# Local maxima of a tile taken in two halves of two score banks, in a kernel of local and routed attention

## The reference

```python
xn = layernorm(x)
# local attention: 16 query heads, 4 key/value heads, rms norm and rope on q and k
q, k, v = xn @ Wq.T + bq, xn @ Wk.T + bk, xn @ Wv.T + bv
q, k = rope(rmsnorm(q, qn_w)), rope(rmsnorm(k, kn_w))
scores = q k^T * scale;  masked where key > query or query - key > 64
local = softmax(scores) v @ Wo.T + bo
# routed attention: one of 16 k/v heads is picked per token by a gate
gating = softmax(xn @ W_gate.T);  idx = argmax(gating);  top = max(gating)
fq, fk, fv = split(xn @ W_qkv.T)
k_shared, v_shared = fk[idx], fv[idx] * top
routed = causal softmax(fq k_shared^T / sqrt(32)) v_shared
out = x + local + routed
```

## Time and profile before

| | us |
|---|---|
| median of 3 runs | 668.64 (667.66 to 670.04) |
| profiled execution, its own time | 671.4 |
| its span | 669.5 |
| PE busy | 637.4 (95%) |
| DVE busy | 455.8 (68%) |
| POOL busy | 442.4 (66%) |
| ACT busy | 361.7 (54%) |
| granted PE clock, mean | 0.993 of full |

### The profile page before, as it was taken

One profiled execution on the slowest core, in us unless ns is written; L12 is line 12 of the kernel. 1 busy time (PEld: TensorE's weight loads), 2 busy tenths in 40 slices (PEclk: granted clock), 3 DMA queues, 4 the chain that ended last, 5 costly groups with the idle time before them and its releaser, 6 DMA issues.

```text
span 669.5 us, 19210 instructions
## 1 busy us (share of the span) xinstructions
PE 637.4 (95%) x7432; PEld 509.8 (76%) x7432; DVE 455.8 (68%) x1184; ACT 361.7 (54%) x906; POOL 442.4 (66%) x384
## 2 busy tenths in 40 slices
PE   4699999999999999999999899999999999999997
PEld 3587788887888888888778677777777777777675
DVE  3966457657665675656664388887878787878454
ACT  5357355625544445535257455656565565656684
POOL 3876856368654749382895467776878687868730
PEclk9999999999999999999999899999999999999999
DMA  9524222241223133212216631503214131302011
GB/s 315 197 60 112 60 77 79 76 122 41 78 70 91 50 94 104 78 39 75 64 33 166 163 96 58 137 26 93 71 51 113 51 111 36 104 29 89 4 34 33
DMA packets 64939, 56.59 MB, mean 85 GB/s; under 512 B 6480, under 2 KB 48848, under 8 KB 64848
## 3 DMA queue, kind: packets, MB, share of 16 engines
q1 hardware_dynamic: 62704, 54.45, 27.9%
q10 hardware_dynamic: 2144, 0.93, 0.5%
HBM read 37.20 MB, written 17.89 MB: 82 GB/s over the span
## 4 chain that ended last, share of the span: by engine, by line
PE 88%; DVE 5%; ACT 2%; DMA 2%; issue 2%; SPq 0%; ACTq 0%; DVEq 0%
PE gemm L946 20%; PE s_ps L1055 12%; PE od_ps L1104 11%; PE st_ps L1088 10%; PE gemm L1032 7%; PE gemm L942 6%; PE od_ps L1118 5%; PE win L1006 4%; PE win L991 3%; PE s_ps L1127 2%; PE av L1018 2%; DMA raw<-w_tok 2%; PE av L1045 1%; PE tp L957 1%; PE tp L913 1%
## 5 line engine op out<-in xcount | busy, mean ns | idle before, releaser
L946 PE MATMUL gemm<-w_tok,xt 128*128 128x512 f32 (+1 forms) x768 | 184.0, 380 | 5.4 <-DVE g_exp L1188 2.2
L946 PEld LDWEIGHTS gemm<-w_tok,xt 128*128 128x128 f32 x768 | 129.6, 191 | 28.5 <-DVE g_exp L1188 2.7
L1055 PE MATMUL s_ps<-k_stack,w_tok 96*128 96x512 f32 (+2 forms) x336 | 100.0, 381 | 0.3 <-DVE x_res L1286 0.3
L1088 PE MATMUL st_ps<-w_tok,k_stack 98*128 98x512 f32 x288 | 98.9, 413 | 0.2 <-ACT p_loc L1545 0.2
L1545 ACT ACTIVATE p_loc<-st_ps 128x512 f32<-128x512 f32 x144 | 77.6, 599 | 35.9 <-PE st_ps L1088 34.7
L1321 DVE TENSOR_REDUCE picked_fk<-s_ps 128x1 f32<-128x512 f32 x112 | 72.3, 684 | 9.0 <-PE s_ps L1055 8.9
L1497 ACT ACTIVATE p_loc<-win,l_max 128x96 f32<-128x96 f32 x256 | 60.9, 390 | 31.1 <-DVE l_max L1260 31.1
L1055 PEld LDWEIGHTS s_ps<-k_stack,w_tok 96*128 96x128 f32 x336 | 54.9, 188 | 24.6 <-issue 8.8
L1642 POOL TENSOR_TENSOR rope_b<-qkv,sin_t 128x128 f32<-128x128 f32 (+1 forms) x32 | 27.5, 880 | 65.5 <-DVE qkv L1238 65.5
L1666 POOL TENSOR_TENSOR p_loc<-p_loc,l_rec 128x1536 f32<-128x1536 f32 x16 | 44.1, 2758 | 36.4 <-DVE l_rec L1272 36.4
L1324 DVE CUSTOM_DVE_ANT_0 s_ps<-s_ps,x_ln,picked_fk 128x128 f32<-128x128 f32 (+3 forms) x112 | 56.8, 555 | 9.7 <-PE s_ps L1055 9.7
(11 more groups left out here) (172 smaller groups left out, 1295.4 us busy)
## 6 DMA issues: line engine op xcount, KB each, us to landing
w_tok<-q_parts SPq DMA_DIRECT2D x72, 128.0 KB, 2.6
q_parts<-qt SPq DMA_DIRECT2D x120, 64.0 KB
x_ln<-x SPq DMA_DIRECT2D x8, 512.0 KB, 4.6
x_res<-x SPq DMA_DIRECT2D x16, 256.0 KB, 2.8
partial<-x_res SPq DMA_DIRECT2D x16, 256.0 KB, 2.3
w_tok<-partial SPq DMA_DIRECT2D x8, 512.0 KB, 5.2
raw<-w_tok SPq DMA_DIRECT2D x3, 1024.0 KB, 12.5
v_win<-v_rows SPq DMA_DIRECT2D x64, 48.0 KB, 2.2
```

Of the source, the lines that this page charges most:

```text
L946: i = e.matmul(g[:, 0:cols], xs[l][:, k, a * P:(a + 1) * P], w_tok_p[r][:, k, c0:c0 + cols], start=first, stop=last)
L1055: e.matmul(s_ps[bank][:, 0:cols], q_op[b][0:HALVES, i, h, :], k_stack[0:HALVES, b * S + c0:b * S + c0 + cols], start=True, stop=True).then ...
L1088: e.matmul(st_ps[k % ST_BANKS][:, :, :], k_stack[0:HALVES + 2, b * S + j * P:b * S + (j + 1) * P], q_op[b][0:HALVES + 2, i, :, :], start=T ...
```

## The change

The `maxima` step of a tile becomes two, each a reduction over two `win` banks into 8 of the 16 columns of `l_max`. The `weights` step becomes two of 8 exponentials each, and each waits only for its own half of the maxima. The step of the second maxima follows the first `weights` step in the list. In the planner's yields a half of the maxima counts 0.9 and a half of the exponentials 2.0 (1.75 and 4.4 for the whole before), and the banks' times in `win_free` follow. Since the planner decides by these times, the order of the whole first stage is another from round 0 on; nothing else is added or removed. From `key_scores` of the first unit on, the order of the second stage is as before.

```diff
--- before.py
+++ after.py
@@ -359,12 +359,16 @@
             win_free[g] = None
         do("scores", m, a)
         yield 1.6, []
-        do("maxima", m, a)
-        yield 0, [("V", 1.75)]
-        do("weights", m, a)
-        def exps_end(end):
-            win_free[:] = [end - 1.1 * (HKV - 1 - g) + HOP for g in range(HKV)]
-        yield 0, [("A", 4.4)], exps_end
+        for half in range(2):
+            do("maxima", m, a, half)
+            yield 0, [("V", 0.9)]
+            do("weights", m, a, half)
+
+            def exps_end(end, half=half):
+                win_free[2 * half:2 * half + 2] = [end - 1.0 + HOP, end + HOP]
+            if half == 0:
+                exps_end(p.busy(p.now, ("A", 2.0)))
+        yield 0, [("A", 2.0)], exps_end
         do("sums", m, a)
         yield 0, [("V", 2.0)]
         do("scaled", m, a)
@@ -1253,13 +1257,13 @@
                                 ALU.subtract).then_inc(*M["gemm_read"].did((n, "qt", c)))
 
             elif step == "maxima":
-                m, a = key
+                m, a, half = key
                 lane.wait_ge(*M["s_mm"].of((m, a)))
                 if m:
                     lane.wait_ge(*M["p_exp"].of((m - 1, a, HKV - 1)))
-                e.tensor_reduce(l_max[:, a, :].rearrange("p (g s) -> p g s", g=HKV),
-                                win[:, :, 0:QUADS * KEYS].rearrange("p g (s k) -> p g s k", s=QUADS), AX.X, ALU.max,
-                                negate=True).then_inc(*M["s_max"].did((m, a)))
+                e.tensor_reduce(l_max[:, a, 2 * QUADS * half:2 * QUADS * (half + 1)].rearrange("p (g s) -> p g s", g=2),
+                                win[:, 2 * half:2 * half + 2, 0:QUADS * KEYS].rearrange("p g (s k) -> p g s k", s=QUADS),
+                                AX.X, ALU.max, negate=True).then_inc(*M["s_max"].did((m, a, half)))
 
             elif step == "sums":
                 m, a = key
@@ -1487,11 +1491,11 @@
                              tp1[0:HALVES, 0:2, :], ACT.Copy).then_inc(*M["fk_out"].did(m))
 
             elif step == "weights":
-                m, a = key
-                lane.wait_ge(*M["s_max"].of((m, a)))
+                m, a, half = key
+                lane.wait_ge(*M["s_max"].of((m, a, half)))
                 if m:
                     lane.wait_ge(*M["pt_mm"].of((m - 1, a, QUADS - 1)))
-                for g in range(HKV):
+                for g in (2 * half, 2 * half + 1):
                     for quad in range(QUADS):
                         n = g * QUADS + quad
                         i = e.activation(p_loc[a][:, g, quad, :], win[:, g, quad * KEYS:(quad + 1) * KEYS], ACT.Exp,
```

## The result

| | before | after |
|---|---|---|
| median, us | 669.34 (667.66 to 671.94, 4 runs) | 681.36 (680.98 to 681.87, 4 runs) |
| profiled execution, its own time | 671.4 | 681.7 |
| its span | 669.5 | 680.5 |

The ratio is 1.0181, with a 95% interval of 1.0156 to 1.0205: 12 us slower. The forecast was 670.7 with a range to 673.4, so it was wrong by far more than its range.

What follows compares the result with a forecast made beforehand. TensorE was taken to bound the first stage. The end's +3.2 (4.4 - 1.2) less the middle's 1.1 gave +2.1 us: 671.4 to 673.5 profiled, 670.7 as median, range 666.8 to 673.4.

Steps and rivals of the forecast that it cites:

- The split itself: Two reductions of 0.95 us for one of 1.76: 2.4 us more VectorE work, all beside TensorE, so 0.
- The middle: First stage, 50 to 350 us: TensorE's waits change by gains 0.2 and 2.9, loss 2.0; gives back 1.1 us.
- The pairs of input and query transposes: Middle, at 77.66 and 167.21: transposes close together in `tp1`; their waits of 1.39 and 1.50 go, gain 2.9 us.
- the first `qt` wait: Middle, at 54.46: a `gemm` waiting 1.28 us for the fourth `qt` copy goes on earlier; gain 0.2 us, not 1.3.
- the wait for `k_stack`: Middle, at 95.53, round 1: the key transpose's wait grows from 0.47 to 1.4 us, 0.9 more.
- the scores of (3, 0): Middle: these come right behind their key transpose, a new close pair costing 0.5 us.
- the `fk_stack` pair of round 5: Middle: transposes with no work before the next user of `tp1`, a new wait of 0.4 us.
- 2 us lost: Worse bound for the middle: old waits go, new waits of the same length come, and none is gained.
- The end, (a): 12 `qt` chunks move ahead of the last query transposes: +4.4 us, to 363.0; rope start moves at most 7.2, not limiting.
- The end, (b): Chain from the last query transposes to the last tile's projection: 23.5 us against 24.7, so -1.2, with the clock falling.
- The sum: Whole kernel: +3.2 at the end of the first stage, -1.1 in the middle, together +2.1 us.
- Rival 1: Faster: banks come free earlier, 5 of the middle's 7.3 us idle go; 666.8 to 665.1 us; chance 0.22.

Runs made afterwards that it cites:

- a1: Changed kernel with both halves kept but planned with the old yields, so every other step keeps the old order; 671.19 us, ratio 1.0021.
- a2: Changed kernel in its new order, with one whole maxima reduction at the first half's place and none at the second; 684.05 us, ratio 1.0213.
- b3: Changed kernel, but the planner keeps the time when bank `tp1` is free and each of its four users waits for it; 668.47 us, ratio 0.9974.
- d1: b3 run once more, unchanged, side by side with d3 and d2; 669.35 us, ratio 0.9986.
- c2: b3 in its own order, with one whole maxima reduction at the first half's place and none at the second; 672.21 us, ratio 1.0034.
- d3: c2 run once more, unchanged, beside d1; 671.74 us, ratio 1.0027.
- b1: Changed kernel, but the planner holds 12 `qt` chunks of round 7 back until the last query transposes are placed; 682.8 us, ratio 1.0188.
- b2: Changed kernel, but the `p_t` steps of tile (6, 0), with its values and projection, wait until the last q product is through; 676.92 us, ratio 1.0109.
- c1: Changed kernel with a half of the maxima counted 0.95, not 0.9, in the planner's yield; same instructions, another order; 675.92 us, ratio 1.0079.
- c3: b3 with a half of the maxima counted 0.95, not 0.9, in the planner's yield; 669.28 us, ratio 0.9981.
- b4: Changed kernel, but the planner holds bank `tp1` back for key transposes alone; 669.18 us, ratio 0.9983.
- d2: b3 with both groups of exponentials waiting for the second half of the maxima; 692.56 us, ratio 1.0341.

## Why the prediction was wrong

**The split itself: 0.** The mechanism and the price were right: the reductions take 0.95 us (0.946 to 0.958), and a1 shows nothing beside them. What I left out is that the split's use depends on the order too: nothing that can be told in the old order, 0.3 to 0.6% in others (the changed kernel against a2, b3 and d1 against c2 and d3). The section of the Trainium skill that I named there (VectorE: DVE Perf Modes, on the trn2 errata) is about operations that read SBUF. These reductions read the PSUM banks `win`, and their fixed part, 0.15 us by the earlier trace rows, is nonetheless of that size.

**The middle: gives back 1.1. This is the first step that failed,** in sign: by idle time alone, from 50 us to the last query transposes, it lost 4.4 (7.3 to 11.7), and 2.5 within the 300 us of the earlier trace rows (7.7 to 10.2). I was right on each wait that I named. The pairs of input and query transposes are gone (no `tp` waits for `xt`), the first `qt` wait is 0.48 and not 1.28, the wait for `k_stack` is 1.61 where I took 1.4, the scores of (3, 0) wait 0.37 (0.5), the `fk_stack` pair of round 5 costs 0.56 (0.4). But I priced a new order by the old list of waits and those pairs in `tp1` that I could see, and left the other idle times "as they are". The new order brought its own: 1.64 at 75.79 and 1.33 at 369.53 for `qt` read late, 0.94 at 236.19, 0.70 to 0.75 at 318.91, 333.80 and 351.15. None is a pair in one bank that an order by itself shows. My bound, "2 us lost", had no row behind it: it let new waits be as long in sum as those I knew.

**The end, (a): +4.4, with GpSimd's rope not setting the time. The second step that failed,** as a cause and not as a sum: the moved chunks are 4.2 us of TensorE's time. But I took the rope's start to move "by at most 7.2 us", the work placed ahead of the q product. It moved by 13.3: 7.2, the 2.0 of the beginning, 2.3 more of idle time of TensorE up to there, and 1.8 that I did not trace. The two ropes take 25 to 26 us in the kernel before, the changed one and b1, so GpSimd reached 370.05 where TensorE reached 371.0. Both paths were late. So b1, without the 4.2 us of chunks, could have won 1.1 at most, and won nothing; b2 and c1, in which the q products stand earlier and the chunks behind as well, won 4.4 and 5.4 by their medians. I had written both paths down as 363.0, equal, and then let every later microsecond count once, on TensorE's side, with the sign of my middle.

**The end, (b): the chain of 23.5. Right:** 23.4. The first `p_t` came 14.05 us behind the transposes (14.2 expected), behind 2.38 us of idle time (about 2), and the granted clock was 0.66 from 386 to 391. That is TensorE at the lower of its two levels for most of that stretch; the mean of 0.66 is near the 0.70 of the earlier trace rows.

**The sum.** It was missed by two steps that work on each other: a middle put at -1.1 was +4.4, and it was passed on in full to an end that had no room, because the q products came later as well. How the 12 us divide between the place of the q products and that of the chunks stays open; that the waits at the banks are about half of them is what c1 and c3 show, by 6.6 us. Rival 1 named the right place with the wrong sign. No rival said that a new order may lose in the middle, though the edit re-plans the whole stage; that case deserved the largest chance beside the forecast.

## What to carry to other kernels

When an edit changes the numbers of a planner, price two things apart: the instructions in the old order (a1, +0.2%), and the order with the old instructions (a2, +2.1%). An order that a planner draws anew is a new draw: 0.05 us in one yield moved this kernel by 1.0%, holding back the key transposes alone by 2.0%; so either keep the old order, or give the planner the resource it does not know (here `tp1`) before reading anything from the time (b3, b4 and c3, three orders, all lie between 0.9974 and 0.9983). And when a reduction is split, the second part goes to wherever the order puts it: what waits for both must stand behind it.

## What the runs showed of the hardware

The beginning is not the same in every execution, in orders that are the same there. GpSimd and VectorE of the changed kernel:

```profile
34.91 3.04 POOL L1630 TENSOR_TENSOR qkv<-qkv,rms_y 128x640 f32<-128x640 f32 x1
```

```profile
34.54 2.29 DVE L1146 TENSOR_TENSOR w_o<-raw,w_o 128x2048 fp32r<-128x2048 f32 x1 [0.95 <-ACT w_o L1402]
```

In b1, whose order is the same up to there, VectorE's operation begins 3 us later, behind GpSimd's:

```profile
34.56 1.27 POOL L1632 TENSOR_TENSOR qkv<-qkv,rms_y 128x640 f32<-128x640 f32 x1
```

```profile
37.60 2.29 DVE L1148 TENSOR_TENSOR w_o<-raw,w_o 128x2048 fp32r<-128x2048 f32 x1 [0.94 <-ACT w_o L1404]
```

GpSimd's operation takes 1.27 us alone. Beside VectorE's it ends 1.12 us behind the end of that one (37.95 against 36.83), about as if it had only begun then. c1, c3, d1 and d2 show the same (3.04 to 3.13 us). The Trainium skill, SBUF — State Buffer, section "SBUF: two separate sides", has this as an exclusive lock: of a VectorE operation with two inputs in SBUF and a GpSimd operation that reads SBUF, the one that starts first holds their shared port pair for its whole length, and the other waits. The trace agrees: VectorE began at 34.54, GpSimd at 34.91.

That it is not the order's doing shows in one program. GpSimd in d1, then in b3, which are the same kernel:

```profile
34.49 3.04 POOL L1643 TENSOR_TENSOR qkv<-qkv,rms_y 128x640 f32<-128x640 f32 x1
```

```profile
34.50 1.26 POOL L1643 TENSOR_TENSOR qkv<-qkv,rms_y 128x640 f32<-128x640 f32 x1
```

At the query transposes of (0, 1) d1 is 2.9 us behind b3 (56.56 against 53.66), at the last ones 1.4 (354.24 against 352.86).

The price is passed on. In the changed kernel the query transposes of (0, 0) waited for this operation:

```profile
38.01 0.94 PE L961 MATMUL tp<-idt,qkv 128*128 128x128 f32 x4 [3.97 <-POOL qkv L1630]
```

From 38 to 56.5 us the granted clock was then 0.91 in the changed kernel, and 1.00 from 36.5 to 53.45 in b1, which had no such wait. By 56 us the changed kernel's profiled execution was 3.1 us behind b1's, and that of the kernel before 1.0 behind a1's, whose order it shares: 3.1 - 1.0 gives the 2.0 (from 3.08 and 1.04) that are not the change's. So the two profiled executions differ by 9 us through the change; the medians differ by 12. How many of the other executions had the collision is not recorded, and whether it is also what spreads the times of one kernel over 4 to 5 us was not tried.
